# Slot inputs rounded by ScalarE instead of VectorE, and the rotary angles moved behind the third value block of the first stage

## The reference

```python
hs = _layernorm(x)
q, k = rope(hs @ Wq.T), rope(hs @ Wk.T)      # 16 heads of 128
v, g = hs @ Wv.T, hs @ Wg.T
s = clip(hs @ Ws1.T @ Ws2.T + bs2, -32, 32)  # 64 slots a head
...
ang = pos[..., :, None] * freqs              # cross attention: cos(ang), sin(ang)
```

## Time and profile before

| | |
|---|---|
| median of 3 runs | 611.94 us (610.56 to 614.62) |
| profiled execution, its own time | 614.3 us |
| its span in the profile | 612.5 us |
| TensorE busy | 95% |
| VectorE busy | 79% |
| ScalarE busy | 60% |
| GpSimd busy | 46% |

### The profile page before, as it was taken

How to read it: one execution, slowest core, us unless ns; L and a number is a source line. 1 busy time by engine, 2 the same in 40 slices (tenths; PEclk the granted TensorE clock), 3 DMA queues, 4 the chain that set the end, 5 groups by cost and what they waited for, 6 DMA issues and landing times.

```text
span 612.5 us, 14139 instructions
## 1 busy us (share of the span) xinstructions
PE 581.9 (95%) x4426; PEld 490.9 (80%) x4426; DVE 486.6 (79%) x1150; ACT 369.8 (60%) x1166; POOL 281.9 (46%) x324
## 2 busy tenths in 40 slices
PE   5989999999999999999999999986889999999998
PEld 5868888888888888888888888774668878877786
DVE  5999978887977977977986986775687887886776
ACT  3448566647657557557567555756666576567453
POOL 3366844754845755663663664545562211220000
PEclk9999999999999999999999999987799999999999
DMA  8200101101100100200200000700000000000000
GB/s 273 70 0 34 55 1 39 50 1 34 51 0 32 54 0 0 86 0 0 86 0 1 18 2 1 276 2 1 3 3 11 2 12 11 3 11 12 3 10 18
DMA packets 10321, 19.35 MB, mean 32 GB/s; under 512 B 2336, under 2 KB 5920, under 8 KB 10144
## 3 DMA queue, kind: packets, MB, share of 16 engines
q1 hardware_dynamic: 10272, 18.74, 8.9%
HBM read 17.55 MB, written 1.05 MB: 30 GB/s over the span
## 4 chain that ended last, share of the span: by engine, by line
PE 81%; DVE 8%; issue 5%; DMA 2%; POOL 1%; ACT 1%; SPq 1%; DVEq 0%; POOLq 0%; ACTq 0%
PE bank L248 16%; PE bank L250 15%; PE bank L249 15%; PE bank L589 4%; PE bank L546 3%; PE bank L1359 3%; PE bank L581 3%; PE bank L558 3%; PE bank L599 2%; PE bank L1288 2%; PE bank L1348 2%; PE bank L1336 2%; PE bank L1407 1%; PE bank L1306 1%; PE bank L1366 1%
## 5 line engine op out<-in xcount | busy, mean ns | idle before, releaser
L845 ACT ACTIVATE sa_v<-bank 128x256 f32<-128x256 f32 x64 | 24.4, 382 | 66.9 <-PE bank L250 66.8
L908 POOL TENSOR_TENSOR sa_qt<-sa_rope_cos,sa_rope_sin 128x512 f32<-128x512 f32 x32 | 41.2, 1286 | 42.2 <-DVE sa_rope_sin L760 42.0
L819 ACT ACTIVATE sa_ex<-sa_okb,sa_minus_top 128x64 f32<-128x64 f32 x128 | 42.9, 339 | 24.9 <-DVE sa_minus_top L712 24.9
L248 PE MATMUL bank<-ht_hi,sa_qk_hi 128*128 128x512 f32 x128 | 55.4, 432 | 1.0 <-DVE sa_gate L765 0.9
L908 POOL TENSOR_TENSOR sa_kt<-sa_rope_cos,sa_rope_sin 128x512 f32<-128x512 f32 x32 | 41.2, 1289 | 30.7 <-DVE sa_rope_sin L760 30.7
L248 PE MATMUL bank<-sa_vg_hi,ht_hi 128*128 128x512 f32 x128 | 52.6, 411 | 0.5 <-DVE sa_rope_sin L760 0.5
L250 PE MATMUL bank<-sa_vg_hi,ht_lo 128*128 128x512 f32 x128 | 50.5, 395 | 0.0
L250 PE MATMUL bank<-ht_hi,sa_qk_lo 128*128 128x512 f32 x128 | 50.5, 394 | 0.0
L249 PE MATMUL bank<-sa_vg_lo,ht_hi 128*128 128x512 f32 x128 | 50.5, 394 | 0.0
L249 PE MATMUL bank<-ht_lo,sa_qk_hi 128*128 128x512 f32 x128 | 50.2, 392 | 0.0
L758 DVE TENSOR_TENSOR sa_rope_cos<-bank,con 128x512 f32<-128x512 f32 x64 | 44.0, 687 | 6.0 <-PE bank L250 5.5
(11 more groups left out here) (207 smaller groups left out, 1840.7 us busy)
## 6 DMA issues: line engine op xcount, KB each, us to landing
sa_qk_raw<-in_wqk SPq DMA_DIRECT2D x8, 512.0 KB, 3.8
sa_vg_raw<-in_wvg SPq DMA_DIRECT2D x8, 512.0 KB, 3.2
sa_wo_raw<-in_wo SPq DMA_DIRECT2D x8, 256.0 KB, 2.7
xf_w_raw<-in_w SPq DMA_DIRECT2D x2, 640.0 KB, 11.1
xf_w_raw<-in_w SPq DMA_DIRECT2D x1, 1152.0 KB, 9.6
xs<-in_x SPq DMA_DIRECT2D x2, 512.0 KB, 4.6
hn<-in_w SPq DMA_DIRECT2D x2, 512.0 KB, 4.9
out<-xs SPq DMA_DIRECT2D x8, 128.0 KB, 1.7
```

The source lines that it names most:

```text
L248: pe.matmul(out, w_hi, m_hi, start=first, stop=False)
L819: ins = act.activation(ex[:, s, u, :], okb[:, s, u, :], ACT.Exp, bias=minus_top[:, s, u:u + 1], accum_out=total[:, g, u:u + 1])
L908: pool.tensor_tensor(dst[:, h, c * HALF:(c + 1) * HALF], rope_cos[:, s, :], rope_sin[:, s, :], ALU.add).then_inc(roped, 1)
```

## The change

The rounding of `u_full` into `us` goes from VectorE to ScalarE, behind ScalarE's L789. VectorE first makes both sums and then both low parts. The first gate (VG 0 of round -1) gets a wait for both low parts, since it overwrites `u_full`. The angles (RA) move in VectorE's list from the first place to the sixth, behind VG 2; RS keeps its place in ScalarE's list, ahead of W2P and behind VG 3.

```diff
-H_DVE = [("RA", 0, -1), ("VG", 0, -1), ("VG", 1, -1), ("QK", 0, -1), ("QK", 1, -1), ("VG", 2, -1), ("VG", 3, -1),
+H_DVE = [("VG", 0, -1), ("VG", 1, -1), ("QK", 0, -1), ("QK", 1, -1), ("VG", 2, -1), ("RA", 0, -1), ("VG", 3, -1),
...
-    u_ready, u_full_done, us_done = sem("u_ready"), sem("u_full_done"), sem("us_done")
+    u_ready, u_full_done, us_hi_done, us_done = sem("u_ready"), sem("u_full_done"), sem("us_hi_done"), sem("us_done")
...
-                        pe.wait_ge(us_done, 4)
+                        pe.wait_ge(us_done, 2)
...
             dve.tensor_scalar(u_full[:, cols], banks[4 + half][:, :], con[:, C_ONE:C_ONE + 1], None, ALU.add).then_inc(u_full_done, 1)
-            dve.wait_ge(u_full_done, half + 1)
-            dve.tensor_copy(us[:, cols], u_full[:, cols]).then_inc(us_done, 1)
-            dve.wait_ge(us_done, 2 * half + 1)
+        for half in range(2):
+            cols = slice(half * HALF, (half + 1) * HALF)
+            dve.wait_ge(us_hi_done, half + 1)
             dve.scalar_tensor_tensor(out=us[:, cols], in0=us[:, cols].bitcast(F32), scalar=con[:, C_LOW_U:C_LOW_U + 1],
                                      in1=u_full[:, cols], op0=ALU.mult, op1=ALU.add).then_inc(us_done, 1)
...
                     dve.wait_ge(th_done, 8 * r + n + 1)
+                    if isinstance(r, int) and r == 0 and n == 0:
+                        dve.wait_ge(us_done, 2)
...
         act.activation(vg_hi[:, :, :], vg_raw[:, :, :], ACT.Copy).then_inc(vg_hi_done, 1)
+        for half in range(2):
+            cols = slice(half * HALF, (half + 1) * HALF)
+            act.wait_ge(u_full_done, half + 1)
+            act.activation(us[:, cols], u_full[:, cols], ACT.Copy).then_inc(us_hi_done, 1)
         act.wait_ge(ws2_done, 1)
```

## The result

The changed kernel is slower: 618.19 us median (4 runs, 617.41 to 621.02) against 611.7 us (4 runs, 610.56 to 614.62), ratio 1.0107, interval 1.0074 to 1.014. That is 6.5 us more, where 3.2 were forecast, and outside the range of 612.2 to 617.8 by 0.4.

The account below looks back on a forecast made before the run. The prediction took VectorE to bound the stage up to about 45 us. Queues, +2.66 us, plus the clock, +0.5, gave +3.2: from 611.94 to 615.1 us, own range 614.6 to 615.6, with spread and nearer rivals 612.2 to 617.8.

Parts of the forecast that it names:

- Parts 1 and 2: Slot inputs and first gates: rounding frees VectorE of 2.28 us, hides in ScalarE's pause; VectorE then idles for two tanhs.
- The gain at VG 1: At VectorE's second joined gate: it starts at 23.64 instead of 24.06, 0.42 us gained from the rounding.
- Part 3: Angles behind VG 2: they delay sine, slot weights' copy and SN 0; TensorE pauses 2.95 us, queues lose 2.66 us.
- Part 4: TensorE's clock after the new pause: a fall likelier than not, costing 0 to 1.0 us on VectorE's chain, taken as 0.5.
- Nothing later gives it back: After SN 0: later TensorE pauses are ended by engines equally late, so the 2.66 us stays.
- a longer fall of the clock: Rival, up to 45 us: nearly all of 13 us at half clock, some 4.7 us lost, 619.3 us; chance 0.08.
- The load of the sine's table: Rival on ScalarE: load starts only once the angles are there, SN 0 1.28 us later, 616.4 us; chance 0.08.
- Other clock falls go away: Rival, cross attention: the shift shortens the half-clock stretch at 422 us, 3.4 us back, 611.7 us; chance 0.10.
- The small gain alone: Rival: SN 0 doesn't wait behind the sine, only late VectorE is left, +1.6 us, 613.5 us; chance 0.04.
- The old rounding: VectorE's first rounding of the slot inputs: read as ending when GpSimd's subtraction is over, at 18.83 us.

Follow-up runs that it names:

- GpSimd held: Changed kernel with GpSimd's addition of QK 1 waiting until the angles are done: 617.46 us, ratio 1.0097.
- With the clock kept as well: Changed kernel with GpSimd's addition of QK 1 waiting for the angles and 12 matmuls without use ahead of SN 0: 614.16 us, ratio 1.0043.
- pause filled: Changed kernel with 16 matmuls without use on TensorE ahead of its wait for the slot weights' copy: 616.36 us, ratio 1.0068.
- the rounding alone: Changed kernel with the angles back first in VectorE's list, only the rounding moved to ScalarE: 611.07 us, ratio 0.9974; again 612.4 us, 0.9998.
- the kernel with the sine later: Changed kernel with the sine behind the slot weights' copy and VG 4 in ScalarE's list: 617.32 us, ratio 1.0053.
- angles after VG 1: Changed kernel with the angles behind VG 1 instead of VG 2 in VectorE's list: 614.32 us, ratio 1.0051.

## Why the prediction was wrong

The direction and the mechanism were right, the size was half: +3.2 against +6.5.

- Parts 1 and 2 hold. The rounding on ScalarE is hidden, the added wait costs nothing, and the gates of VG 0 and VG 1 wait for their tanhs. The gain at VG 1 was put at 0.42. Over the stage it is 0.23, and in the time it can't be seen.
- Part 3, "2.00 us of the queue and 2.09 us until the last is done", was carried to the new place unchanged. That is the first mis-sized term: 2.83 us of the queue there (28.61 to 31.44) and 2.92 until the last is done, because one multiplication is held by GpSimd and takes 0.99 us. I had weighed just such a hold for the low parts of the slot inputs, and not for the angles, though GpSimd's addition of QK 1 ran from 28.68 us in the trace before and would start 0.4 sooner, beside them:

```profile
28.68 1.29 POOL L908 TENSOR_TENSOR sa_kt<-sa_rope_cos,sa_rope_sin 128x512 f32<-128x512 f32 x1 [0.77 <-DVE sa_rope_sin L760]
```

- The rest of part 3 holds as it stands. With GpSimd held, the pause is 2.85 us and SN 0 is clipped at 31.87 (32.05 once the start of the stage is set equal), for 2.95 and 31.96 forecast. With the clock kept as well, the stage is 2.79 us late, for 2.66.
- Part 4, the clock at +0.5 between bounds of 0 and 1.0, is the second and larger term that was mis-sized. It measured 2.2 us (changed kernel less pause filled). The bound failed in two places. I took the 3.4 us of the fall at 404 us for the length of this one; it was 6.8 here, 5.1 of them under matmuls, with a pause of 3.68 us, and 3.4 with one of 2.85. And I took TensorE's wait of 0.85 us as slack that half clock would use up first. But VectorE waits for TensorE before that. It clips SN 0 right behind TensorE, 0.47 us later than in the filled kernel once the starts are set equal, and waits another 0.16 for SN 1. Then its gates of VG 5 and VG 6 wait 0.24 and 1.30 us for tanhs that ScalarE computes only after TensorE's late ST 1; in the filled kernel neither gate waits. These four make 2.2 us. The sum had a slip besides: after the 0.3 taken back, 0.55 of the 0.85 remains and not 0.7, which would make the upper bound 1.15; it doesn't reach 2.2 either.
- So the 5.89 us are: 2.66 as summed (2.79 measured), 0.9 from the held multiplication and what hangs on it (3.67 - 2.79), and 2.2 from the clock (5.89 - 3.67). The two interact: a longer pause brought the longer fall, and holding GpSimd alone gave 1.66 back.
- "Nothing later gives it back" holds up to the cross attention: 5.98 us late at the matmuls on `xf_h`, 5.89 at the first mask. The 0.6 between the stage and the medians is within the medians' uncertainty.
- Of the rivals, "a longer fall of the clock" was the nearest: its kind came, at half of its 13 us. The load of the sine's table ran ahead of the wait, as argued, at 26.39, and the tanh behind the second load began 1.29 us after it (32.30 and 33.59), so no drain shows here either. "Other clock falls go away" came in part in the profiled pair, where the falls near 405 and 566 us are missing after the change; that such falls come and go without the change is seen from the rounding alone: of its two profiled executions, the same kernel, the clock fell behind this wait of 1.24 us in one and not in the other (0.89 and 1.00 from 400 to 416 us). "The small gain alone" missed that VectorE's late queue brings a pause of its own: in the kernel with the sine later TensorE paused 3.26 us at QK 5, and its clock fell as well. Its median came out 4.7 above its own runs of before, where +1.6 was the rival's price.
- The old rounding was read as ending with GpSimd's subtraction. It ended at 19.11, 0.28 us behind it (18.83). Nothing in the sum rests on that.

## What to carry to other kernels

In this kernel a piece of work that filled a wait cost nothing, and the same piece a few entries later cost its length, the pause of whoever waited for its result, and what the paused TensorE lost by its clock. Before moving it, ask what its queue was waiting for at the old place, who stands behind the reader of its result, and what its neighbour on the shared ports does at the new one. If TensorE pauses for 3 us, price the clock by the work that lies between the pause and the next engine that waits for TensorE, and don't count slack that comes later.

## What the runs showed of the hardware

- The clock: TensorE paused 3.68 us and had 6.8 us at 1.2 GHz, from 2.0 us into the pause on; pauses of 2.85 and 3.26 us were followed by 3.4 us, which began 0.7 to 0.9 us after matmuls ran again. After 1.38 us among matmuls (angles after VG 1) the profile has none in the stage. The pause alone doesn't decide it: behind the same wait of 1.24 us near 405 us the clock fell for 3.4 us in the kernel before and not in the changed one, and in one of the two executions of the rounding alone. Matmuls without use in the pause kept the clock at 2.4 GHz, and that was worth 2.2 us of the 5.9.
- One 128x4 multiplication of VectorE with two inputs in SBUF took 989 ns instead of 155 while GpSimd added 128x512 values, and ended 0.03 us after GpSimd did. The old rounding, 1.85 us instead of 0.43, had ended 0.28 us after GpSimd's subtraction.
- ScalarE's table load started while the instruction behind it was still waiting for its semaphore, 5.17 us ahead of it (26.39 and 31.56). The load was over at 27.67, well within the wait.
